# Row 1's causal convolution on TensorE with diagonal matrices, its B/C projection behind the first feature maps

## The chip, the core and the metric

The program runs on one core of a Trainium2 chip. Its engines are TensorE (PE, matrix products into PSUM), VectorE (DVE), ScalarE (ACT), GpSimd (POOL) and SyncE (SP, which here only starts DMAs). Each engine works through its own queue in order; semaphores tie the queues together. The time is the device time of one execution in microseconds (us), and each comparison takes the median of several.

## What is computed

A decoder layer on `x` (4, 512, 512) with three residual parts: linear attention with 16 heads, a selective state-space mixer (as in Mamba) that reads `ctx_1024` (4, 512, 256) and is gated by the normalized `x`, and a feed-forward part with 8-bit activations and ternary weights. The change is in the front of the mixer:

```python
x = jnp.einsum('bld,ed->bel', hidden_states, in_proj_w)            # (4, 512, 512)
xc = conv_general_dilated(x, conv_w, window_strides=(1,), padding=[(3, 0)],
                          feature_group_count=512)                 # 4 taps, one filter per channel
x = silu(xc + conv_b[None, :, None])                               # "U" in the kernel
x_dbl = jnp.einsum('bdl,ed->bel', x, x_proj_w)                     # 16 + 16 + 16 rows
dt_low, Bm, Cm = jnp.split(x_dbl, [16, 32], axis=1)
dt = softplus(jnp.einsum('brl,dr->bdl', dt_low, dt_proj_w) + dt_proj_b[None, :, None])
# scan over time: state = state * exp(dt * A) + (dt * x) * B;  y = (state * C).sum() + D * x
```

## The kernel before

The batch has four rows, b = 0 to 3, and everything is laid out with channels on the 128 partitions and the 512 time steps along them, so that a tensor of 512 channels is four tiles (e = 0 to 3). The mixer's scan is cut into 32 units per row, each for one state n and one half h of the channels: TensorE spreads the row of B over all partitions into PSUM (`spread_b`), VectorE multiplies it by DU (`inputs_b`) and scans (`scan`), ScalarE makes the decays exp(dt A) for it ahead of time (`decay`), GpSimd multiplies by the row of C, adds two units of row 0 together and starts a DMA that accumulates them into ACC (`outputs_c`). These units run through the whole kernel; tables written out by hand (`STEP_PIECES`, `STEP_DECAYS`, `STEP_SPREADS`) say at which named point of an engine's program how many of them are placed. Between them stand the attention of row b (`attention`, four groups g of four heads) and the feed-forward part of row b - 1. In row 0, ScalarE also forms absolute sums of 24 pieces of the feed-forward weights and makes them ternary.

The front of the mixer for row b is: `xin` (the input projection, four products of two 128x512 matmuls each), `tap` on ScalarE (the last tap and the bias, from PSUM into U), `conv` on VectorE (three `scalar_tensor_tensor` per tile, which read the product in PSUM and accumulate in U), `silu_u` on ScalarE, `xdbl` on TensorE (the 48 rows of B, C and the low-rank step size), `x_proj` on ScalarE (which drains them) and, at the end of the row, `step_size` and `step_inputs` (DU = DT x U, on GpSimd). Row 0's front opens the kernel. Row 1's stands in row 0, ahead of its attention: TensorE's `first_row` issues `xin(1, e)`, two spreads, `xdbl(1)` and then `attention(0)`; ScalarE's issues `tap(1, e)`, three decays and two weight sums, `silu_u(1, e)`, a load of the table for exp and ln, `skip_term(1, 0)`, `x_proj(1)` and then `attention(0)`; VectorE's `STEP_PIECES[0]` puts the twelve steps of `conv(1, e)` between units 3 to 5. Rows 2 and 3 have their front inside the feed-forward part of the row before.

Every product has a PSUM bank and two counting semaphores (class `Banks`): TensorE waits until the bank's last reader has drained it. The bank is the one least recently used in the order of `all_products`. DU and the diagonal's input IDF (the identity) and CW (the taps) are in SBUF. ARENA is a scratch region; columns 0 to 2047 of it hold QT, KTT, T1 and T2 of the attention, which nothing writes before the first `first_factor`.

At the start of the kernel GpSimd computes the four tiles of DU of row 0 and then waits for unit 0; VectorE meanwhile cuts B into three bf16 parts (`split_first`, lines 1915 to 1924), normalizes the rows of x (`normed`, line 1879) and begins with the units. The transposes of the normalized rows (`normed_T`, line 916) wait for all four tiles.

Of the kernel before, what the change touches and what calls it, by code (L numbers as in the profile page):

```python
# [19 lines left out]
ALU = mybir.AluOpType  # L20
# [3 lines left out]
P = 128  # L24
# [9 lines left out]
TAPS = 4  # L34
# [88 lines left out]


def front_products(b):
    return [(b, "xin", e) for e in range(KT)] + [(b, "xdbl")]

# [18 lines left out]
def attention_products(b):  # L146

    out = []
    for g in range(first_group(b), GROUPS):
        out += [(b, m, g) for m in ("q1", "q2", "k1", "k2")]  # L150
        if g + 1 < GROUPS:
            out += [(b, "q", g + 1)]
        if g > first_group(b):
            out += [(b, "ms", g - 1)]
        if b + 1 < BATCH and g == 2:
            out += [(b + 1, "dt", 0), (b + 1, "dt", 1)]
        out += [(b, "kfT", g), (b, "S", g, 0), (b, "S", g, 1), (b, "kv", g)]
        if b + 1 < BATCH and g == GROUPS - 1:
            out += [(b + 1, "xnT", k) for k in range(KT)]
        if b == 0 and g == 1:  # L160
            out += [(0, "gsum")]
        if g + 1 < GROUPS:
            out += [(b, "k", g + 1)]
        out += [(b, "o", g), (b, "S", g, 2), (b, "S", g, 3)]
        if g + 1 < GROUPS:
            out += [(b, "v", g + 1)]
    return out
# [341 lines left out]
def decoder_layer(nc, x, ctxT, wqT, wkT, wvT, woT, fmaps, fbias, normw, inT, convw, convb, xpT, dtpT, dtb, alog,  # L509
                  dskip, wffn, ffbias, outb, ident, ident16, id96, causal, headones, out, parts):  # L510
    ctx = ExitStack()
    with ctx:
# [112 lines left out]
        HT = part(3072, 1024, bf16).rearrange("p (k t) -> p k t", k=HK)  # L625
        HALVES = [part(off, 1024) for off in (4096, 5120, 0)]


# [63 lines left out]
        conv_step = signal("conv_step", KT * (TAPS - 2))  # L692
        u_ready = signal("u_ready", KT)
        split_step = signal("split_step", 4)
        bc_parts = signal("bc_parts", 32)
# [32 lines left out]
        hr_ready = signal("hr_ready", 2 * TT)  # L728
        bias_added = signal("bias_added", 1)

        block = ctx.enter_context(nc.Block())
# [138 lines left out]
        def _(pe):  # L870
# [21 lines left out]
            def xin(b, e):  # L892
# [3 lines left out]
                        [ctx_loaded.at(b)])  # L896

            def xdbl(b):
                key = (b, "xdbl")
                product(key, over_k(R.bank(*key)[0:2 * N + RANK, :], [(WXP[:, k, :], U[:, k, :]) for k in range(KT)]),  # L900
                        [u_ready.at(b)])

# [243 lines left out]
            def attention(b):  # L1146
                for g in range(first_group(b), GROUPS):
# [11 lines left out]
                    if b + 1 < BATCH and g == 2:  # L1159
                        step_size(b + 1, 0)  # L1160
                        step_size(b + 1, 1)
                    units(b, "a", g, 2)
                    keys_T(b, g)
# [19 lines left out]
            def first_row():  # L1183
# [19 lines left out]
                units(0, "r", 3)  # L1203
                xdbl(1)
                pe.wait_ge(setup_v, SETUP_V)
# [109 lines left out]
        def _(act):  # L1315
# [4 lines left out]
            def tap(b, e):  # L1320

                act.wait_ge(*R.full_at(b, "xin", e))
                if e == 0 and b:
                    act.wait_ge(*du_ready.at(b - 1))
                act.activation(U[:, e, :], R.bank(b, "xin", e)[:, :], ACT.Identity, bias=CB[:, e:e + 1],  # L1325
                               scale=CW[:, e, TAPS - 1:TAPS]).then_inc(tap_done.sem, 1)

            def silu_u(b, e):
                act.wait_ge(*R.drained_at(b, "xin", e))
                act.activation(U[:, e, :], U[:, e, :], ACT.Silu).then_inc(u_ready.sem, 1)  # L1330
# [47 lines left out]
            def skip_term(b, h):  # L1378

                act.wait_ge(*u_ready.at(b))  # L1380
                if h and b:
                    act.wait_ge(*yg_ready.at(b - 1))
                for i in range(2):
                    e = 2 * h + i
                    act.activation(ACC[(2 * b + h) % 3][:, i, :], U[:, e, :], ACT.Identity, scale=DSK[:, e:e + 1])\
                       .then_inc(y_init.sem, 1)
# [158 lines left out]
            def attention(b, f):  # L1545
                for g in range(first_group(b), GROUPS):
# [19 lines left out]
                    if g == 1 and f is not None:  # L1566
                        act.wait_ge(*R.full_at(f, "O", TT - 1))
                    keys_rows(b, g)
                    decays(b, "a", g, 3)
# [11 lines left out]
            def first_row():  # L1581
# [28 lines left out]
                for e in range(KT):  # L1610
                    tap(1, e)
                decays(0, "r", 3)
# [3 lines left out]
                skip_term(1, 0)  # L1616
                x_proj(1)
                attention(0, None)
# [127 lines left out]
        def _(pool):  # L1746
# [30 lines left out]
            def step_inputs(b, e):  # L1777

                pool.wait_ge(*R.drained_at(b, "dt", e))
                if b:  # L1780
                    pool.wait_ge(*dbu_done.at(0, half_units(b - 1, e // 2)[-1] + 1))
                pool.wait_ge(*u_ready.at(b, e + 1))
                pool.tensor_tensor(DU[:, e, :], DT[:, e, :], U[:, e, :], ALU.mult).then_inc(du_ready.sem, 1)  # L1783

            def split(b):
# [8 lines left out]
                pool.tensor_tensor(BC1, BCR, BC2, ALU.subtract).then_inc(split_step.sem, 2)  # L1794

            for e in range(KT):
                step_inputs(0, e)
            for u in range(TOTAL):
                outputs_c(u)
# [17 lines left out]
        def _(dve):  # L1817
# [80 lines left out]
            def conv(b, e, row=None):  # L1898

                x_in = R.bank(b, "xin", e)  # L1900
                for s in range(1, TAPS):
                    units(row, "c", e, s)
                    if s == 1:
                        dve.wait_ge(*tap_done.at(b, e + 1))
                    else:
                        dve.wait_ge(*conv_step.at(b, e * (TAPS - 2) + s - 1))
                    ins = dve.scalar_tensor_tensor(U[:, e, s:], x_in[:, 0:L - s], CW[:, e, TAPS - 1 - s:TAPS - s],  # L1907
# [522 lines left out]
```

## Time and profile before

| | |
|---|---|
| median of 3 runs | 935.37 us (933.5 to 935.75) |
| the profiled execution | 929.06 us, span 927.3 us |
| TensorE busy | 788.3 us (85%) |
| VectorE busy | 770.0 us (83%) |
| ScalarE busy | 596.8 us (64%) |
| GpSimd busy | 489.6 us (53%) |
| mean granted clock of TensorE | 0.936 |

Busy times overlap, and a wait counts only where nothing else is late at its place. A row of the timeline gives the start, the busy time from there to the end of the last merged instruction, the engine, the line in the kernel, the operation, the tile written and the tiles read, the number of instructions, and in brackets the idle time before it with what ended it. An f32 matmul has two records in the trace, so "x8" of `MATMUL ... f32` are four matmuls. The granted clock 1.00 is 2.4 GHz and 0.50 is 1.2 GHz.

### The profile page before, as it was taken

What the parts mean: (1) busy time and instruction counts of PE and PEld (TensorE: products, weight loads), DVE (VectorE), ACT (ScalarE), POOL (GpSimd) and SP (SyncE); (2) the same over time, 40 slices, a digit from 0 to 9 for tenths busy, and PEclk for the clock granted to TensorE, in tenths of its full rate; (3) what the DMA queues carried; (4) which work ended last, traced back from release to release, by engine and by line L of the source; (5) the groups of instructions that cost most, each with busy time, mean ns of one, the idle gap of its engine ahead of it and who ended that gap; (6) DMA issues with size and microseconds to landing.
All of it is one profiled execution on the core that took longest, in us unless ns stands there. A gap on an engine that the chain in (4) does not pass through costs nothing. (4 is left out here: it accounts for less than half of the span.)

```text
span 927.3 us, 11769 instructions
## 1 busy us (share of the span) xinstructions
PE 788.3 (85%) x4070; PEld 427.9 (46%) x4070; DVE 770.0 (83%) x948; ACT 596.8 (64%) x900; POOL 489.6 (53%) x292
## 2 busy tenths in 40 slices
PE   5859998369788898998987887998889899999798
PEld 1334555143453334665453334655446335664343
DVE  5987778996998985989589988689778998987875
ACT  3888899975746956455466966463466786454553
POOL 0456678787656523575447643276453745565020
PEclk9989997679999999999989999999998999999999
DMA  8697788876545535567635663456653565666000
GB/s 292 255 250 230 213 261 230 236 189 170 121 103 122 114 69 114 138 145 174 127 69 120 121 134 69 125 120 147 159 107 81 117 129 125 153 143 137 0 12 35
DMA packets 50783, 131.12 MB, mean 141 GB/s; under 512 B 7299, under 2 KB 7875, under 8 KB 50725
## 3 DMA queue, kind: packets, MB, share of 16 engines
q0 software_dynamic: 16128, 58.73, 33.5%
q1 hardware_dynamic: 34596, 71.65, 23.9%
q8 instruction: 33, 0.54, 0.2%
q14 instruction: 26, 0.21, 0.1%
HBM read 67.09 MB, written 4.35 MB: 77 GB/s over the span
## 5 line engine op out<-in xcount | busy, mean ns | idle before, releaser
L1762 POOL TENSOR_TENSOR W<-W,CROW 128x1024 f32<-128x1024 f32 x128 | 322.6, 2537 | 158.7 <-DVE W L1951 131.7
L1951 DVE TENSOR_TENSOR_SCAN W<-DEC,PB 128x1024 f32<-128x1024 f32 x125 | 285.1, 2281 | 11.2 <-ACT DEC L1375 3.1
L1775 POOL DMA_DIRECT2D ACC<-W x112 | 98.5, 879 | 153.9 <-DMA ACC<-W 130.2
L1940 DVE TENSOR_TENSOR PB<-DU,PB 128x1024 f32<-128x1024 f32 x128 | 156.5, 1223 | 13.2 <-PE PB L1070 11.6
L1375 ACT ACTIVATE DEC<-DT,ACOL 128x511 f32<-128x511 f32 x250 | 160.1, 711 | 10.3 <-DVE W L1951 10.2
L1126 PE MATMUL bank<-W,ARENA 128*128 128x512 fp8e4 x512 | 125.2, 389 | 0.0
L1318 ACT ACTIVATE ARENA<-bank 128x512 f32<-128x512 f32 x56 | 32.6, 592 | 72.5 <-PE bank L886 34.8
L1126 PEld LDWEIGHTS bank<-W,ARENA 128*128 128x128 bf16 x512 | 45.6, 99 | 61.8 <-issue 17.9
L1479 ACT ACTIVATE ARENA<-bank,SDQ 128x512 f32<-128x512 f32 x64 | 43.2, 686 | 43.4 <-PE bank L1126 43.1
L1070 PE MATMUL PB<-BC,ID 96*128 96x512 bf16 x98 | 38.6, 408 | 34.2 <-DVE W L1951 32.8
L2093 DVE SCALAR_TENSOR_TENSOR ARENA<-bank,SDQ,ARENA 128x512 f32<-128x512 f32 x64 | 47.3, 743 | 17.5 <-PE bank L1126 6.4
L886 PE MATMUL bank<-XNT,WQ 128*128 128x512 f32 x128 | 61.6, 626 | 0.1
L948 PEld LDWEIGHTS bank<-WV,XNT 128*128 128x128 f32 x512 | 60.4, 195 | 2.7 <-issue 2.2
L1983 DVE TENSOR_TENSOR ARENA<-bank,CAUSAL 128x512 f32<-128x512 f32 x64 | 42.5, 680 | 22.3 <-PE bank L987 22.2
L886 PE MATMUL bank<-XNT,WK 128*128 128x512 f32 x128 | 60.0, 613 | 1.2 <-DVE ARENA L1983 1.1
L948 PE MATMUL bank<-WV,XNT 128*128 128x128 f32 x512 | 61.0, 278 | 0.0
L1142 PE MATMUL bank<-W,ARENA 128*128 128x512 fp8e4 x256 | 57.9, 379 | 0.0
L1119 PE MATMUL bank<-BROW,RT 32*128 32x512 bf16 x128 | 29.5, 385 | 22.6 <-DVE ARENA L2093 12.4
L1468 ACT ACTIVATE ARENA<-bank 128x512 bf16<-128x512 int16 x76 | 40.5, 593 | 11.2 <-PE bank L928 11.2
L1907 DVE SCALAR_TENSOR_TENSOR U<-bank,CW,U 128x511 f32<-128x511 f32 (+2 forms) x48 | 35.4, 746 | 14.1 <-ACT U L1325 12.8
L1783 POOL TENSOR_TENSOR DU<-DT,U 128x512 f32<-128x512 f32 x16 | 22.9, 1509 | 45.2 <-ACT DT L1355 45.2
L886 PE MATMUL bank<-ARENA,FM 128*128 128x512 f32 x96 | 45.2, 600 | 0.6 <-DVE LOW L2170 0.4
(185 smaller groups left out, 1339.3 us busy)
## 6 DMA issues: line engine op xcount, KB each, us to landing
ACC<-W POOLq DMA_DIRECT2D x112, 512.0 KB, 4.6
CROW<-c_rows SPq DMA_DIRECT2D x98, 256.0 KB, 3.6
W<-in_wffn SPq DMA_DIRECT2D x27, 512.0 KB, 6.1
X<-in_wffn SPq DMA_DIRECT2D x21, 512.0 KB, 5.4
X<-in_x SPq DMA_DIRECT2D x7, 1024.0 KB, 8.2
out_dram<-X SPq DMA_DIRECT2D x16, 256.0 KB, 2.2
X<-in_ctxT SPq DMA_DIRECT2D x4, 512.0 KB, 5.5
ARENA<-in_x SPq DMA_DIRECT2D x1, 1024.0 KB, 5.5
```

What stands on the lines that cost most here:

```text
L886: last = pe.matmul(o, lhs, rhs, start=start, stop=n == len(terms) - 1)
L948: last = pe.matmul(o[:, t * P:(t + 1) * P], XNT[:, k, t * P:(t + 1) * P], WV[:, k, g * P:(g + 1) * P], start=k == 0, stop=k == KT - 1)
L1126: last = pe.matmul(o, XQT[:, k, t * P:(t + 1) * P], w, start=False, stop=k == KT - 1)
L1142: last = pe.matmul(o, HT[:, k, :], W8[:, 2 * WPC + k // 2, (k % 2) * 512:(k % 2) * 512 + 512], start=k == 0, stop=k == HK - 1)
L1375: last = act.activation(to[:, i, 1:], DT[:, e, 1:], ACT.Exp, scale=ACOL[:, e, n:n + 1])
L1479: act.activation(G[n % 2], R.bank(f, "G", t, c)[:, :], ACT.Silu, scale=SDQ[:, 0, t:t + 1])\
L1762: pool.tensor_tensor(w, w, CROW[k % 2][:, :].unsqueeze(1).broadcast_to([P, 2, L]), ALU.mult)\
L1775: pool.dma_start(ACC[accumulator(u)][:, :, :], w, accum_op=ALU.add).then_inc(y_summed, 16)
L1940: dve.tensor_tensor(into, du, rows, ALU.mult).then_inc(dbu_done.sem, 1)
L1951: dve.tensor_tensor_scan(flat(W[u % 4]), flat(decay_of(u)), flat(PB[:, scan_bank(u):scan_bank(u) + 2, :]), 0.0, ALU.mult, ALU.add).then_in ...
L1983: dve.tensor_tensor(homes(b, g)["st"][c % 2].rearrange("p (h q) -> p h q", h=HPG), R.bank(b, "S", g, c)[:, :].rearrange("p (h q) -> p h q" ...
L2093: dve.scalar_tensor_tensor(h, R.bank(f, "V", t, c)[:, :], SDQ[:, 1, t:t + 1], G[(t * HC + c) % 2], ALU.mult, ALU.mult)\
```

## The change

Row 1's convolution leaves VectorE. Before the first unit, GpSimd multiplies the identity by each tap of each channel: DIAG holds 16 diagonal matrices, in four instructions of 128x512. ScalarE copies the input projection from PSUM to U without tap and bias (`conv_input`). TensorE then forms the convolution of each tile as four f32 products of a diagonal matrix with U, each shifted by one more step, into one PSUM bank. `silu_u` reads that bank and adds the bias in the same instruction. `xdbl(1)` stands on TensorE behind the four feature maps and the `q` projection of group 0 (which is for group 1), and `x_proj(1)` on ScalarE ahead of `keys_rows` of group 0. Rows 0, 2 and 3 are as before.

```diff
+CONV_ON_PE = 1
 def front_products(b):
-    return [(b, "xin", e) for e in range(KT)] + [(b, "xdbl")]
+    out = [(b, "xin", e) for e in range(KT)]
+    if b == CONV_ON_PE:
+        return out + [(b, "conv", e) for e in range(KT)]
+    return out + [(b, "xdbl")]
...
@@ attention_products
+        if b == 0 and g == 0:
+            out += [(1, "xdbl")]
         out += [(b, "kfT", g), (b, "S", g, 0), (b, "S", g, 1), (b, "kv", g)]
...
+        DIAG = part(0, KT * TAPS * P).rearrange("p (e w c) -> p e w c", e=KT, w=TAPS)
...
@@ TensorE
+            def conv(b, e):
+                key = (b, "conv", e)
+                o = R.bank(*key)
+                product(key, [(o[:, s:], DIAG[:, e, TAPS - 1 - s, :], U[:, e, 0:L - s], s == 0) for s in range(TAPS)],
+                        [(diag_made, KT), R.drained_at(b, "xin", e)])
...
@@ attention
+                    if b == 0 and g == 0:
+                        xdbl(1)
                     units(b, "a", g, 2)
                     keys_T(b, g)
...
@@ first_row
                 units(0, "r", 3)
-                xdbl(1)
+                for e in range(KT):
+                    conv(1, e)
                 pe.wait_ge(setup_v, SETUP_V)
                 attention(0)
...
@@ ScalarE
+            def conv_input(b, e):
+                if e == 0:
+                    act.wait_ge(*du_ready.at(b - 1))
+                drain((b, "xin", e), U[:, e, :], R.bank(b, "xin", e)[:, :])
+
             def silu_u(b, e):
+                if b == CONV_ON_PE:
+                    act.wait_ge(*R.full_at(b, "conv", e))
+                    act.activation(U[:, e, :], R.bank(b, "conv", e)[:, :], ACT.Silu, bias=CB[:, e:e + 1])\
+                       .then_inc(R.drained(b, "conv", e), 1)
+                    return
...
@@ attention
+                    if b == 0 and g == 0:
+                        x_proj(1)
                     keys_rows(b, g)
...
@@ first_row
                 for e in range(KT):
-                    tap(1, e)
+                    conv_input(1, e)
                 decays(0, "r", 3)
...
                 skip_term(1, 0)
-                x_proj(1)
                 attention(0, None)
...
@@ GpSimd
+            def diagonals(e):
+                if e == 0:
+                    pool.wait_ge(w_conv, W_CONV)
+                    pool.wait_ge(w_misc, W_MISC)
+                pool.tensor_tensor(DIAG[:, e, :, :], IDF[:, :].unsqueeze(1).broadcast_to([P, TAPS, P]),
+                                   CW[:, e, :].unsqueeze(2).broadcast_to([P, TAPS, P]), ALU.mult).then_inc(diag_made, 1)
             for e in range(KT):
                 step_inputs(0, e)
+            for e in range(KT):
+                diagonals(e)
             for u in range(TOTAL):
...
@@ VectorE, conv
                 for s in range(1, TAPS):
                     units(row, "c", e, s)
+                    if b == CONV_ON_PE:
+                        continue
```

The remaining lines replace waits on `u_ready` of row 1 by waits on the drained banks of its `conv` products, and count the semaphores of the other rows' convolutions without row 1.

## Rows read from the trace of the kernel before

**Rows 1.** Timeline of VectorE, 50 to 81 us (columns as told above).

```profile
50.36 1.23 DVE L1940 TENSOR_TENSOR PB<-DU,PB 128x1024 f32<-128x1024 f32 x1 [2.90 <-PE PB L1070]
...
68.48 2.29 DVE L1951 TENSOR_TENSOR_SCAN W<-DEC,PB 128x1024 f32<-128x1024 f32 x1
...
75.23 0.75 DVE L1970 SCALAR_TENSOR_TENSOR ARENA<-bank,FB,ARENA 128x512 f32<-128x512 f32 x1 [4.47 <-PE bank L886]
...
80.82 1.23 DVE L1940 TENSOR_TENSOR PB<-DU,PB 128x1024 f32<-128x1024 f32 x1 [0.74 <-PE PB L1070]
```

**Rows 2.** Timeline of TensorE's products, 56 to 81 us.

```profile
56.96 0.60 PE L1070 MATMUL PB<-BC,ID 96*128 96x512 bf16 x2
...
67.38 5.84 PE L886 MATMUL bank<-U,WXP 128*48 128x512 f32 x8 [9.82 <-ACT U L1330]
...
73.14 1.98 PE L886 MATMUL bank<-X,FM 128*128 128x512 f32 x4
...
76.90 3.60 PE L886 MATMUL bank<-XNT,WQ 128*128 128x512 f32 x8
...
80.33 0.38 PE L1070 MATMUL PB<-BC,ID 96*128 96x512 bf16 x1
```

**Rows 3.** Stretches: us, busy us of PE, PEld, DVE, ACT, POOL; clock, DMA share, GB/s.

```profile
36.00:51.00 15.00, 13.73 (x69) 8.81 (x68) 11.96 (x9) 14.87 (x27) 9.06 (x4) 1.00 0.58 187
...
61.60:71.80 10.20, 4.42 (x6) 1.17 (x7) 9.03 (x8) 8.28 (x13) 5.15 (x4) 0.50 0.86 231
...
80.00:212.00 132.00, 98.35 (x573) 62.14 (x572) 114.84 (x99) 119.30 (x162) 102.56 (x55) 0.83 0.81 229
...
201.60:211.70 10.10, 5.84 (x21) 2.91 (x22) 8.16 (x6) 7.89 (x8) 7.50 (x4) 0.50 0.75 220
```

**Rows 4.** Timeline of ScalarE, 65 to 75 us.

```profile
65.14 2.19 ACT L1330 ACTIVATE U<-U 128x512 f32<-128x512 f32 x4
...
68.64 1.33 ACT L1385 ACTIVATE ACC<-U,DSK 128x512 f32<-128x512 f32 x2
...
73.74 0.57 ACT L1318 ACTIVATE XBC<-bank 48x512 f32<-48x512 f32 x1
...
74.31 0.69 ACT L1410 ACTIVATE ARENA<-bank,FBS 128x512 f32<-128x512 f32 x1
```

**Rows 5.** Timeline of VectorE, 10 to 36 us.

```profile
10.75 8.99 DVE L1907 SCALAR_TENSOR_TENSOR U<-bank,CW,U 128x511 f32<-128x511 f32 x12 [9.35 <-ACT U L1325]
...
27.68 0.41 DVE L1919 CAST X<-X 32x512 bf16<-32x512 f32 x1
...
28.84 1.25 DVE L1922 COPY BC<-X 32x512 bf16<-32x512 bf16 x1
...
30.10 1.39 DVE L1924 CAST BC<-X 32x512 bf16<-32x512 f32 x1
...
32.98 2.55 DVE L1879 TENSOR_SCALAR ARENA<-ARENA,MV,RSTD 128x512 f32<-128x512 f32 x4 [0.23 <-ACT RSTD L1349]
```

**Rows 6.** Timeline of GpSimd, 28 to 47 us.

```profile
28.46 2.74 POOL L1783 TENSOR_TENSOR DU<-DT,U 128x512 f32<-128x512 f32 x2 [28.02 <-ACT DT L1355]
...
31.17 2.71 POOL L1783 TENSOR_TENSOR DU<-DT,U 128x512 f32<-128x512 f32 x2
...
40.55 5.68 POOL L1762 TENSOR_TENSOR W<-W,CROW 128x1024 f32<-128x1024 f32 x2 [6.67 <-DMA CROW<-c_rows]
```

**Rows 7.** Timeline of VectorE and of GpSimd, 242 to 248 us.

```profile
242.90 3.42 DVE L2165 TENSOR_TENSOR ARENA<-ACC,ARENA 128x1024 f32<-128x1024 f32 x2
...
243.32 4.13 POOL L1783 TENSOR_TENSOR DU<-DT,U 128x512 f32<-128x512 f32 x2 [2.63 <-ACT DT L1355]
```

**Rows 8.** Timeline of TensorE's products, 34 to 40 us.

```profile
35.59 1.97 PE L916 MATMUL bank<-IDF,ARENA 128*128 128x128 f32 x16 [1.02 <-DVE ARENA L1879]
...
39.05 0.39 PE L1070 MATMUL PB<-BC,ID 96*128 96x512 bf16 x1 [1.27 <-DVE W L1951]
```

**Rows 9.** Timeline of VectorE at 216 us.

```profile
216.00 0.69 DVE L1990 TENSOR_TENSOR OT<-bank,OT 128x512 f32<-128x512 f32 x1 [4.97 <-ACT OT L1423]
```

More of the change, by code:

```diff
@@ L122, in quarters, with conv_rows @@
     return (2 * half, 2 * half + 1)
+CONV_ON_PE = 1
 def front_products(b):
-    return [(b, "xin", e) for e in range(KT)] + [(b, "xdbl")]
+    out = [(b, "xin", e) for e in range(KT)]
+    if b == CONV_ON_PE:
+        return out + [(b, "conv", e) for e in range(KT)]
+    return out + [(b, "xdbl")]
+def conv_rows(b):
+    return b - (b > CONV_ON_PE)
 SCALE_GROUPS = ((0, 1), (1, 2), (2, 3), (3, 4))
@@ L693, in decoder_layer @@
         u_ready = signal("u_ready", KT)
+        diag_made = once("diag_made")
         split_step = signal("split_step", 4)
@@ L729, in decoder_layer, with conv_done @@
         bias_added = signal("bias_added", 1)
+        def conv_done(b, n=KT):
+            if b == CONV_ON_PE:
+                return R.all_drained_at(*((b, "conv", e) for e in range(n)))
+            return [u_ready.at(conv_rows(b), n)]
         block = ctx.enter_context(nc.Block())
@@ L900, in xdbl @@
                 product(key, over_k(R.bank(*key)[0:2 * N + RANK, :], [(WXP[:, k, :], U[:, k, :]) for k in range(KT)]),
-                        [u_ready.at(b)])
+                        conv_done(b))
             def step_size(b, e):
@@ L1378, in skip_term @@
             def skip_term(b, h):
-                act.wait_ge(*u_ready.at(b))
+                for r in conv_done(b):
+                    act.wait_ge(*r)
                 if h and b:
@@ L1781, in step_inputs @@
                     pool.wait_ge(*dbu_done.at(0, half_units(b - 1, e // 2)[-1] + 1))
-                pool.wait_ge(*u_ready.at(b, e + 1))
+                for r in conv_done(b, e + 1):
+                    pool.wait_ge(*r)
                 pool.tensor_tensor(DU[:, e, :], DT[:, e, :], U[:, e, :], ALU.mult).then_inc(du_ready.sem, 1)
@@ L1902, in conv @@
                     units(row, "c", e, s)
+                    if b == CONV_ON_PE:
+                        continue
                     if s == 1:
-                        dve.wait_ge(*tap_done.at(b, e + 1))
+                        dve.wait_ge(*tap_done.at(conv_rows(b), e + 1))
                     else:
-                        dve.wait_ge(*conv_step.at(b, e * (TAPS - 2) + s - 1))
+                        dve.wait_ge(*conv_step.at(conv_rows(b), e * (TAPS - 2) + s - 1))
                     ins = dve.scalar_tensor_tensor(U[:, e, s:], x_in[:, 0:L - s], CW[:, e, TAPS - 1 - s:TAPS - s],
```

## The prediction

> **What bounds the kernel now.** I read the changed place first on VectorE, then TensorE, then ScalarE, in the timelines of 50 to 81 us, and after that asked what the new GpSimd work meets in the first 40 us. VectorE is the busiest engine after TensorE, but look at what ends its idle time. It runs the convolution of row 1 between the mixer's units, finishes its last unit of the block at 70.77 us and then stands still for 4.47 us until TensorE has the first feature map [rows 1]. Later it waits 0.74 us for the spread of B of unit 7. TensorE in turn stands still for 9.82 us before the projection to B and C, which then takes 5.84 us for four products [rows 2], since its granted clock is 0.50 (1.2 GHz) from 61.6 to 71.8 us, 4 us into that wait [rows 3]. What ends TensorE's wait is the last `silu_u`, itself behind VectorE's last tap. So a chain convolution (VectorE), SiLU (ScalarE), B/C projection and first map (TensorE) sets this place. ScalarE lies just beside it: a table load (the 1.3 us between its last SiLU and its skip terms) and 1.33 us of skip terms run under the projection, and it comes to `first_factor` at 74.31 us [rows 4].
>
> **What goes.** Twelve VectorE instructions, 8.99 us in row 0's identical convolution [rows 5]. All of them fall before 65 us, in a stretch whose end is a 4.47 us wait for another engine, so by themselves they are worth nothing: without them VectorE's units 4 and 5 are done near 64.5 us (unit 4's spread comes at 57.4, then two products and two scans, 1.23 + 2.29 us each) and it waits some 11 us instead of 4.5.
>
> **What the chain becomes.** A group of four f32 products of 128x512 goes from start to start in 3.43 us at full clock (76.90 to 80.33 us [rows 2]); the new `conv` is four such groups, 511 to 509 columns in three of four, so 13.7 us. The last spreads before it end at 57.4 us, the first input is in U by then (a copy like the one that drains XBC, 0.57 us [rows 4]), so TensorE runs 57.4 to 71.1 us without a gap and at full clock. The last SiLU can start at 71.3 and takes 0.65 us (2.19 for four [rows 4]); the load and the skip terms, formerly hidden under the projection, now follow it: 71.95 + 1.3 + 1.33 = 74.6 us for `first_factor`, against 74.31. VectorE's first map comes at 75.3 instead of 75.23. Nothing is gained there: TensorE is 2 us earlier (71.1 against 73.14), ScalarE 0.3 later, and the later one decides.
>
> TensorE next does the four feature maps (to 74.7 us) and the projection `q` of group 1. It takes the bank of q1, which `first_factor` frees at 75.3 us: 75.3 + 3.43 = 78.7. Then comes the moved projection, 3.43 us at full clock, to 82.15; and only behind it, in TensorE's queue, the spread for unit 7, the transposes of the keys, the scores and kv. Before, that spread started at 80.33 us. VectorE waited for it already (0.74 us), so it is late by 82.15 - 80.33 = **1.8 us**. On ScalarE, `x_proj` (two instructions, 1.1 us) waits for the moved product and holds `keys_rows`, three decays and nine weight sums behind it, 2.2 us late; the first of these decays belongs to unit 8, whose scan lies a whole unit behind the late spread, so 1.8 stays. From 80 to 212 us VectorE is busy for 114.8 of 132 us and ScalarE for 119.3 [rows 3], and what they wait for is on engines that are shifted alike, so I carry 1.8 us to the end. B and C themselves are asked for by `split` behind unit 9 and by the step sizes of group 2: hidden. No DMA moves; `store_c(1)` stands late in the queue of SyncE.
>
> **The diagonals.** GpSimd forms DIAG in four instructions of 128x512 behind its four DU products. It is idle from 33.88 to 40.55 us [rows 6], and four at 1.36 us (2.74 for two) seem to fit. But see what VectorE does there. The same small cast takes 0.41 us alone, and 1.25 and 1.39 us while GpSimd multiplies DU [rows 5, 6]; the two engines take turns. The same at 243 us: two VectorE products of SBUF operands need 3.42 us instead of 2.46 (2 x 1.23, a product of that size [rows 1]), two GpSimd products 4.13 instead of 2.74 [rows 6, 7]. Just where the diagonals start, VectorE normalizes row 0 (`normed`, four TENSOR_SCALAR of 128x512, 2.55 us from 32.98 [rows 5]). Its first one already waits for the last DU. The next three would each find a diagonal in front: from the casts, 0.84 and 0.98 us each; from [rows 7], 3.42 - 2.46 = 0.96. I take three times 1.0, so 3.1 us with hand-over; the bounds are 0 (VectorE always served first) and 3 x 1.31 = 3.9 (a whole GpSimd instruction each).
>
> The Trainium skill says in "GPSIMD Engine Reference", section "Key points", that GpSimd shares its SBUF interfaces with VectorE and collides with instructions in a 2-port mode or with two SBUF inputs; "VectorE: DVE Perf Modes", section "Mode 2×_2P", makes f32 `tensor_scalar` such a one. The trace agrees (0.41 against 1.25 and 1.39 us). Neither gives a price; by them the port term stands, and by GpSimd's idle time alone it would be 0 and the time 937.2.
>
> That delay has no cover. The transposes of row 0 wait for all four normalized tiles, VectorE's first unit is queued behind them, TensorE waits 1.27 us for that first scan at 39.05 us [rows 8], then works through q, k and v without a gap, and VectorE waits 2.90 us for the spread behind v at 50.36 [rows 1]. So 3.1 us pass on to the start of `conv`. TensorE's idle time before the transposes grows from 1.02 to 4.1 us [rows 8]. In the wait from 57.56 us the clock fell after 4 us and stayed at 0.50 for 10.2 us [rows 2, 3]; here too a stretch at 1.2 GHz may come. It costs nothing, or up to 1.7 us if 3.4 us of q and k run at half clock. I take 0.6, nearer to nothing because TensorE works again at once.
>
> **The sum.** 1.8 + 3.1 + 0.6 = 5.5 us. The profiled execution (929.06 us, span 927.3) would become 934.6. It was 0.7% faster than the median of the three runs, 935.37; the shift is the same there: **940.9 us**. With the bounds of the unknown terms: 1.8 + 0 + 0 = 1.8 to 1.8 + 3.9 + 1.7 = 7.4, so 937.2 to 942.8.
>
> **Rivals.**
> - *The diagonals cost nothing.* GpSimd takes its turn only when VectorE asks for none; the four are done before its first C product. For it: two of VectorE's normalizations in a row ran undisturbed, but nothing of GpSimd's was queued then. Then only the moved projection counts: 937.2 us, no change that can be told. It decides where fewer than one of the three turns goes to GpSimd (1.8 + 1.0 = 2.8 us, which is 0.3% and about what a measurement of this kernel can tell from no change).
> - *Given back by the clock.* Row 0's end has a stretch at 0.50 from 201.6 to 211.7 us [rows 3], behind which VectorE waits 4.97 us for the RMS of the last heads [rows 9]. A shifted program meets the clock otherwise; if TensorE is at full speed there, at most 4.97 us come back. With 1.8 that is 932.2 us, faster; with 5.5 it is 935.9. Against it: that stretch begins in waits of TensorE for scans, which the change leaves.
> - *It does less harm or more by ScalarE.* If the copies and SiLUs of row 1 come late behind the normalization's delay (ScalarE is busy for 14.9 of 15 us from 36 to 51 us [rows 3]), the chain grows by another 1 to 2 us: 942.5.
> - *The products take one pass.* If the diagonal products ran at 0.43 instead of 0.86 us each, `conv` would end at 64.3, ScalarE at 70.1 for `first_factor`, and the spread of unit 7 would come 2.6 us early; with the diagonals' 3.1 that is 935.9. Every f32 product of 512 columns in the trace has two records and 0.86 us, so I give it little.
>
> **Chances.** Forecast 0.57 (about 939 to 942.5), diagonals free 0.20, clock gives back 0.11, later ScalarE 0.09, one pass 0.03. Of the clock's 0.11 some 0.07 end faster by over 0.3%, of the forecast's some 0.02 fall within 0.3%. That makes faster 0.07, same 0.28, slower 0.65. The range for 8 in 10 reaches from inside the free and clock cases to the ScalarE case: 935.5 to 943.0.
>
> **What would show it.** Right: `normed` of row 0 with three instructions of 1.4 to 1.6 us each, and the first scan ending near 42.1 instead of 39.05; TensorE without a gap from the four `xin` to the last `conv`, ending 21 us after the first `xin` starts; VectorE idle for about 11 us before its first feature map; the spread of unit 7 behind the moved projection, and 5 to 6 us on the start of row 1. Wrong: `normed` at 2.6 us in all (then 937); `first_factor` far ahead of the last `conv` plus 3.3 us; or row 0's later waits on DMA and ACC sums shrinking by microseconds, which would mean that the shift is absorbed.

## The result, and the profile after

| | before | after |
|---|---|---|
| median (lowest to highest) | 932.02 us (928.72 to 936.99, 18 runs) | 938.05 us (930.37 to 943.76, 18 runs) |
| ratio of after to before | | 1.0067, 95% interval 1.0048 to 1.0085 |
| the profiled execution | 929.06 us, span 927.3 | 943.76 us, span 941.6 |
| TensorE, VectorE busy | 788.3, 770.0 us | 808.0, 767.3 us |

The change makes the kernel some 6 us slower. The forecast was 940.9 us (935.5 to 943.0) and a shift of 5.5 us. The profiled execution of after is the slowest of its 18. VectorE's first unit starts at 40.29 us in it instead of 35.46, and some of that was late before any new instruction ran: DU's first product starts at 29.91 us instead of 28.46 [rows 6]. So the places are compared by intervals from one unit of VectorE to another (u3 is its fourth unit), and the starting stretch by a second series of the same kernel, **change_again**.

First the changed place. Timeline of TensorE after, 55 to 89 us; it answers to [rows 2]:

```profile
55.60 7.03 PE L907 MATMUL bank<-X,WIN 128*128 128x512 f32 x16
...
62.90 13.86 PE L907 MATMUL bank<-U,ARENA 128*128 128x512 f32 x32
76.59 1.88 PE L907 MATMUL bank<-X,FM 128*128 128x512 f32 x4
...
80.84 3.67 PE L907 MATMUL bank<-XNT,WQ 128*128 128x512 f32 x8 [0.43 <-ACT ARENA L1451]
84.45 3.63 PE L907 MATMUL bank<-U,WXP 128*48 128x512 f32 x8
88.01 0.39 PE L1097 MATMUL PB<-BC,ID 96*128 96x512 bf16 x1
```

The second row is the convolution: 16 products, 32 records, 0.86 us each as forecast. No row down to the feature maps has an idle time; in the window below TensorE is busy for all of it, at full clock. Then ScalarE, 76 to 89 us; it answers to [rows 4]:

```profile
76.80 0.69 ACT L1366 ACTIVATE U<-bank,CB 128x512 f32<-128x512 f32 x1 [2.74 <-PE bank L907]
77.50 1.28 ACT L1565 ACT_TABLE_LOAD   x1
78.79 1.33 ACT L1426 ACTIVATE ACC<-U,DSK 128x512 f32<-128x512 f32 x2
80.03 0.67 ACT L1451 ACTIVATE ARENA<-bank,FBS 128x512 f32<-128x512 f32 x1
...
88.12 0.59 ACT L1582 ACTIVATE BC<-bank 32x512 bf16<-32x512 f32 x1 [1.92 <-PE bank L907]
```

The feature maps are long done when ScalarE comes to `first_factor`: last SiLU, table load and skip terms stand in a row, all behind the last product. VectorE, 55 to 89 us; it answers to [rows 1]:

```profile
55.87 1.23 DVE L1995 TENSOR_TENSOR PB<-DU,PB 128x1024 f32<-128x1024 f32 x1 [3.31 <-PE PB L1097]
...
80.73 0.75 DVE L2025 SCALAR_TENSOR_TENSOR ARENA<-bank,FB,ARENA 128x512 f32<-128x512 f32 x1 [10.65 <-ACT ARENA L1451]
...
88.51 1.23 DVE L1995 TENSOR_TENSOR PB<-DU,PB 128x1024 f32<-128x1024 f32 x1 [2.93 <-PE PB L1097]
```

VectorE is rid of 9 us of work and stands still for 10.65 us instead of 4.47. From the spread that starts u3 to the first feature map it takes 24.86 us (55.87 to 80.73); before it was 24.87 (50.36 to 75.23 [rows 1]). From u3 to u7 it takes 32.64 us instead of 30.46. That is the interval on which most of what follows rests, because it holds the whole changed place and starts at the same point in every kernel.

Now the start, in change_again: timelines of VectorE, GpSimd and TensorE, 33 to 46 us. They answer to [rows 5], [rows 6] and [rows 8]:

```profile
33.37 4.71 DVE L1932 TENSOR_SCALAR ARENA<-ARENA,MV,RSTD 128x512 f32<-128x512 f32 x4 [0.23 <-ACT RSTD L1389]
38.01 1.22 DVE L1995 TENSOR_TENSOR PB<-DU,PB 128x1024 f32<-128x1024 f32 x1
```

```profile
34.22 4.76 POOL L1844 TENSOR_TENSOR ARENA<-IDF,CW 128x512 f32<-128x512 f32 x4
```

```profile
38.14 3.48 PE L943 MATMUL bank<-IDF,ARENA 128*128 128x128 f32 x16 [3.04 <-DVE ARENA L1932]
...
42.51 3.67 PE L907 MATMUL bank<-XNT,WQ 128*128 128x512 f32 x8 [0.45 <-ACT XNT L1348]
```

The four normalizations take 4.71 us instead of 2.55, TensorE waits 3.04 us for them instead of 1.02, and its 16 transposes take 3.48 us instead of 1.97. The view of that line, in ns (least, median, most), shows each of them held up:

```profile
L1932 DVE TENSOR_SCALAR ARENA<-ARENA,MV,RSTD x4: 1178/1256/1257, 33.4 to 36.8; 128x512 f32<-128x512 f32 x4
```

The same view of before, where only the first one stands beside GpSimd:

```profile
L1879 DVE TENSOR_SCALAR ARENA<-ARENA,MV,RSTD x4: 533/534/1182, 33.0 to 35.0; 128x512 f32<-128x512 f32 x4
```

A normalization beside nothing adds 0.46 us there ((2.55 - 1.18) / 3; each starts a little before the last has ended). In change_again each of these three adds 1.18 us ((4.71 - 1.18) / 3).

Windows of after; columns as in [rows 3]:

```profile
40.31:43.73 3.42, 3.30 (x16) 3.31 (x17) 3.39 (x3) 1.64 (x3) 0.00 (x0) 0.50 0.30 88
43.73:56.00 12.27, 11.82 (x54) 7.26 (x53) 8.41 (x8) 12.04 (x22) 9.11 (x4) 1.00 0.47 138
55.60:76.80 21.20, 21.20 (x52) 9.51 (x51) 10.54 (x6) 13.49 (x24) 12.68 (x6) 1.00 0.82 232
```

The transposes run at 1.2 GHz behind TensorE's wait (4.18 us in this execution); from the projection q on the clock is whole again.

### The profile page after: what moved, and what is told of

Same layout as the page of the kernel before. It is cut to its first block, busy times and chain, and to the rows that moved or that the text cites. A ratio compares the mean times of both kernels' runs of the same rounds, so it can differ in the third digit from the quotient of the medians.

```text
span 941.6 us, 11838 instructions
## 1 busy us (share of the span) xinstructions
PE 808.0 (86%) x4102; PEld 438.8 (47%) x4102; DVE 767.3 (81%) x936; ACT 596.7 (63%) x900; POOL 493.6 (52%) x296
## 4 chain that ended last, share of the span: by engine, by line
PE 46%; DVE 25%; issue 11%; ACT 9%; POOL 4%; DMA 4%; DVEq 0%; SPq 0%; POOLq 0%; ACTq 0%
PE bank L907 18%; DVE W L2006 8%; PE bank L1153 6%; DVE PB L1995 4%; PE bank L1054 4%; PE bank L975 3%; DMA ACC<-W 3%; PE bank L1169 3%; POOL W L1804 3%; PE bank L1014 2%; PE bank L1037 2%; PE bank L996 2%; DVE HAM L2156 1%; DVE ARENA L2148 1%; PE bank L943 1%
## 5 line engine op out<-in xcount | busy, mean ns | idle before, releaser
L907 PE MATMUL bank<-XNT,WK 128*128 128x512 f32 x128 | 62.1, 631 | 3.2 <-DVE ARENA L2038 3.1
L1054 PE MATMUL bank<-WO,OT 128*128 128x512 f32 x96 | 46.1, 635 | 2.6 <-DVE OT L2045 2.6
```

The costliest lines, as they stand in the source:

```text
L907: last = pe.matmul(o, lhs, rhs, start=start, stop=n == len(terms) - 1)
L1054: pe.matmul(R.bank(*key)[:, :], OT[:, k, t * P:(t + 1) * P], WO[:, k, :], start=k == 0, stop=False, skip_group_check=True)
```

## The experiments

Each kernel ran in five rounds beside the kernel before. There were three series: diag_only, diag_early, pe_later_early and maps_first in the first; change_again, diag_late, move_only and move_later in the second; the rest, on another chip, in the third. "Ratio" is against before of the same series, with its 95% interval, as recorded; it is not the quotient of the two medians and can differ from it by up to 0.002. The medians of before were 931.19, 932.46 and 931.92 us. Intervals are read from VectorE's timeline of one profiled execution.

| kernel | median us | ratio | u0 to u3 | u3 to u7 | u3 to u32 |
|---|---|---|---|---|---|
| before | | | 14.90 | 30.46 | 155.97 |
| after | 938.05 | 1.0067 (1.0048 to 1.0085) | 15.58 | 32.64 | 158.81 |
| change_again | 939.9 | 1.008 (1.0046 to 1.0113) | 15.50 | 32.64 | 158.84 |
| diag_only | 935.52 | 1.0043 (1.0015 to 1.0071) | 15.44 | 30.99 | 158.45 |
| diag_early | 936.66 | 1.0059 (1.0031 to 1.0086) | 14.90 | 32.64 | 159.15 |
| diag_late | 937.47 | 1.0048 (1.0022 to 1.0074) | 14.90 | 32.64 | 158.78 |
| pe_later_early | 936.56 | 1.0056 (1.0035 to 1.0077) | 15.97 | 29.64 | 158.77 |
| pe_stay_early | 936.11 | 1.0037 (1.0012 to 1.0062) | 14.91 | 33.08 | 158.22 |
| conv_short | 930.59 | 0.9983 (0.996 to 1.0006) | 14.99 | 28.21 | 154.31 |
| move_only | 928.07 | 0.9958 (0.9934 to 0.9982) | 14.91 | 28.77 | 152.95 |
| move_only_2 | 930.35 | 0.9975 (0.9953 to 0.9997) | 14.91 | 28.79 | 154.23 |
| move_later | 930.15 | 0.9958 (0.9936 to 0.998) | 14.90 | 25.08 | 156.20 |
| maps_first | 929.41 | 0.9983 (0.9963 to 1.0004) | 16.09 | 28.10 | 154.29 |
| maps_first_warm | 931.1 | 0.9987 (0.9962 to 1.0013) | 15.92 | 27.89 | 153.87 |

**diag_only.** The kernel before with the four diagonal products at the place of the change; nothing reads them.

```diff
             for e in range(KT):
                 step_inputs(0, e)
+            for e in range(KT):
+                diagonals(e)
```

> The kernel before plus the four GpSimd instructions for the diagonals, at the place where the change puts them; nobody reads them (ScalarE only waits for them before the attention), and the convolution stays on VectorE. My theory: they take turns with VectorE's normalization, which lasts 5 to 6 us instead of 2.55, TensorE goes idle for 4 us, and the time is 3 to 4 us above the kernel before (ratio 1.003 to 1.005). Rival (GpSimd is idle there, so they cost nothing): ratio 1.000.

The normalizations again take 4.71 us:

```profile
33.88 4.71 DVE L1892 TENSOR_SCALAR ARENA<-ARENA,MV,RSTD 128x512 f32<-128x512 f32 x4 [0.23 <-ACT RSTD L1351]
```

The time is 1.0043 of before. Four instructions that no one needs cost about 4 us (1.4 to 6.6 by the interval), and the profile shows 2.7 of them: 2.16 in the normalizations and 0.54 from u0 to u3, where the transposes ran at half clock. "Diagonals cost nothing" falls. The ratio is the expected one, but the four normalizations (4.71 us) and TensorE's wait (3.04 us) are below the 5 to 6 and the 4 us expected. This profile is also 0.53 us longer from u3 to u7 and 1.95 from there to u32 than that of before, where the edit adds nothing but a wait that has long been met; what takes these 2.5 us was not followed up.

**diag_early** and **diag_late.** The change with the diagonals ahead of DU, while GpSimd waits for DT; and with GpSimd waiting for `normed` before them.

```diff
-            for e in range(KT):
-                step_inputs(0, e)
             for e in range(KT):
                 diagonals(e)
+            for e in range(KT):
+                step_inputs(0, e)
```

```diff
                     pool.wait_ge(w_conv, W_CONV)
                     pool.wait_ge(w_misc, W_MISC)
+                    pool.wait_ge(*xn_ready.at(0))
```

> The changed kernel with the four diagonals ahead of the four DU products instead of behind them, where VectorE normalizes nothing. My theory: the 3 to 4 us of the turns go, the moved projection's 1.8 to 2.2 us stay: ratio to the kernel before 1.002 to 1.0025. Rival (all of the loss is in the moved projection and the convolution): ratio stays at 1.006 to 1.007.

> The changed kernel, with GpSimd waiting for the four normalized tiles before its first diagonal, so that nothing takes turns. The diagonals early left a ratio of 1.006, more than my sum had. Theory A (the turns cost 3 us, and the rest of the change 2.2 us as the spread of unit 7 shows; the ratio of the early diagonals lay high within its uncertainty): ratio 1.002 to 1.004, and unit 7 2.2 us later against unit 3 than in the kernel before. Theory B (the convolution on TensorE and the moved projection cost some 5 us in all, part of it later in row 0): ratio 1.005 to 1.006 again.

Timelines of VectorE of diag_early, and of VectorE and GpSimd of diag_late:

```profile
34.05 2.54 DVE L1932 TENSOR_SCALAR ARENA<-ARENA,MV,RSTD 128x512 f32<-128x512 f32 x4 [0.23 <-ACT RSTD L1389]
```

```profile
33.67 2.54 DVE L1933 TENSOR_SCALAR ARENA<-ARENA,MV,RSTD 128x512 f32<-128x512 f32 x4 [0.23 <-ACT RSTD L1389]
36.14 1.21 DVE L1996 TENSOR_TENSOR PB<-DU,PB 128x1024 f32<-128x1024 f32 x1
```

```profile
36.38 4.04 POOL L1845 TENSOR_TENSOR ARENA<-IDF,CW 128x512 f32<-128x512 f32 x4 [1.82 <-DVE ARENA L1933]
```

In both the last three normalizations are undisturbed and u0 to u3 is 14.90 us as before. In diag_late GpSimd multiplies beside VectorE's products and scans, and VectorE's 1.21 us product and u0 to u3 do not grow. That product reads DU from SBUF and PB from PSUM. The Trainium skill ("GPSIMD Engine Reference", section "Key points") names as contending VectorE's instructions in a 2-port mode or with two SBUF inputs; this trace agrees, with one SBUF input and no loss here. diag_late is 2.4 us faster than change_again, its neighbour on the same chip (939.9 against 937.47; the two intervals overlap), where the profile has 2.76 us (2.16 + 0.60). So by the profiles the place of the diagonals is worth 2 to 3 us. The ratios of the change with and without turns don't separate it: 1.0067 and 1.008 against 1.0059 and 1.0048, all intervals overlapping. Both kernels remain at 1.005 to 1.006, about 5 us that are not the turns'. The expectation of diag_early (1.002 to 1.0025) missed this, and that of diag_late is split: unit 7 is 2.18 us late as in theory A, the ratio is nearer to theory B.

**move_only**, **move_only_2.** The kernel before with nothing but the moved projection, the convolution on VectorE; two series.

```diff
@@ attention, TensorE
+                    if b == 0 and g == 0:
+                        xdbl(1)
                     units(b, "a", g, 2)
@@ first_row, TensorE
-                xdbl(1)
@@ attention, ScalarE
+                    if b == 0 and g == 0:
+                        x_proj(1)
                     keys_rows(b, g)
@@ first_row, ScalarE
-                x_proj(1)
```

> Only the second half of the change: the convolution stays on VectorE and there are no diagonals, but row 1's B/C projection and its drain stand where the change puts them (behind the q projection). Theory A (the loss of the change at this place is the 13.7 us chain of products followed by SiLU, table load and skip terms, and the move by itself gains): VectorE gets its first map without a wait, unit 7 is 2 to 2.5 us earlier against unit 3, ratio 0.997 to 0.999. Theory B (it is the moved projection ahead of the spread of unit 7 that loses): 1.8 to 2.2 us slower, ratio 1.002.

> The kernel before with nothing but the projection to B and C moved to the place of the change (TensorE: behind the feature maps and the q projection; ScalarE: ahead of the rows of the keys); a second series of the same kernel, beside the others of this call. Theory A (the move by itself gains 3 to 4 us, since the first feature maps no longer wait for a projection at half clock): ratio 0.994 to 0.998. Rival B (the first series was chance): 0.999 to 1.001.

Timelines of move_only, TensorE, and of move_only_2, VectorE:

```profile
68.05 3.62 PE L888 MATMUL bank<-X,FM 128*128 128x512 f32 x4
71.46 4.08 PE L888 MATMUL bank<-XNT,WQ 128*128 128x512 f32 x8
75.47 3.63 PE L888 MATMUL bank<-U,WXP 128*48 128x512 f32 x8
79.04 0.39 PE L1072 MATMUL PB<-BC,ID 96*128 96x512 bf16 x1
```

```profile
71.12 0.72 DVE L1974 SCALAR_TENSOR_TENSOR ARENA<-bank,FB,ARENA 128x512 f32<-128x512 f32 x1
...
75.22 0.72 DVE L1974 SCALAR_TENSOR_TENSOR ARENA<-bank,FB,ARENA 128x512 f32<-128x512 f32 x1
79.58 1.23 DVE L1944 TENSOR_TENSOR PB<-DU,PB 128x1024 f32<-128x1024 f32 x1 [3.63 <-PE PB L1072]
```

The moved projection alone makes the kernel faster: 0.9958 and 0.9975, some 2 to 4 us, both intervals below 1. The first feature map comes with no wait and 4.5 us earlier (20.33 us behind u3, 71.12 - 50.79, instead of 24.87). Of that 2.9 are lost again at the spread of unit 7, which now stands behind the projection (3.63 us of waiting), and 1.7 us stay (30.46 - 28.78), somewhat less than the 2 to 2.5 expected. The projection now takes 3.63 us instead of 5.84; the slow stretch has gone over to the two feature maps and to q (3.62 and 4.08 us). This is one half of the change, and the better half.

**move_later**, **pe_later_early.** The projection one step further down, behind the projection k of group 1: once with the convolution on VectorE, once with it on TensorE (diagonals early).

```diff
                         qk(b, "k", g + 1)
+                    if b == 0 and g == 0:
+                        xdbl(1)
                     attend(b, g, 0)
```

> The kernel before with row 1's B/C projection moved further, behind the k projection of group 1; convolution on VectorE, no diagonals. Theory A: the spread of unit 7 comes right behind the q projection, VectorE's wait for it (2.95 us with the maps first) goes, and the projection costs 1.5 us at unit 10: 3 to 4 us faster than before, ratio 0.996 to 0.997. Rival (the projection delays the second pair of scores as much as it gave back): ratio 0.998, as with the maps first.

> As diag_early, and row 1's B/C projection moved on from ahead of the keys' transposes to behind the k projection of group 1 (its drain on ScalarE alike), where TensorE waits 1.7 us for a masked score. My theory: the spread of unit 7 is no longer behind the projection, so VectorE reaches it up to 0.6 us earlier than in the kernel before, the projection costs about 1 us later: ratio 1.000 to 1.001. Rival (the convolution on TensorE itself delays the chain, wherever the projection stands): as diag_early or above, 1.002.

VectorE no longer waits for the spread of unit 7, and u3 to u7 falls to 25.08 and 29.64 us, 3.7 and 3.0 us less than with the projection at the place of the change. The ratios gain nothing: 0.9958 and 1.0056, as their partners have (pe_later_early was expected at 1.000 to 1.001, a miss). In the profile of move_later the interval from u7 to u12 is 23.00 us instead of before's 21.05, and that from u12 to u32 108.11 instead of 104.45. Of the first, 1.5 us lie at the spread of unit 10, which stands behind the projection now, as expected (u9 to u10 6.48 us instead of 5.01):

```profile
89.88 1.23 DVE L1944 TENSOR_TENSOR PB<-DU,PB 128x1024 f32<-128x1024 f32 x1 [2.46 <-PE PB L1072]
```

So in this profile the gain at unit 7 is handed back before row 1; what takes the rest was not isolated. One execution does not carry the median here: this one has a longer u3 to u32 and a longer span (928.3 us) than the profiled execution of before (927.3), while the ratio over 12 runs is 0.9958.

**maps_first**, **maps_first_warm.** The kernel before with the projection between the four feature maps and the projection q; the second with 34 small products that keep TensorE busy in its wait.

```diff
                     units(b, "a", g, 1)
+                    if b == 0 and g == 0:
+                        xdbl(1)
                     if more:
                         qk(b, "q", g + 1)
```

> The kernel before with only its order changed: the convolution stays on VectorE, the B/C projection of row 1 goes behind the four feature maps of group 0 and ahead of the q projection, its drain on ScalarE alike; no diagonals. My theory: VectorE no longer waits 4.5 us for the first map, and the projection runs in TensorE's idle time; the spread of unit 7 comes 2.3 us earlier than before (TensorE at 1.2 GHz for part of it): ratio 0.997 to 0.998. Rival (the gain of an earlier first map is lost because TensorE then does projection and q in a row): ratio 1.000.

> The kernel before with the projection to B and C between the four feature maps and the projection q of group 1, the convolution on VectorE, and 34 keep-busy products of TensorE ahead of the feature maps, in its wait for the last spreads. Theory A (the half clock of the projection behind a wait of 9.8 us costs here): the maps and the projection run at 1.00, unit 3 to 7 is 1 to 2 us shorter than the 28.1 us without the keep-busy products, ratio 0.994 to 0.997. Rival B: the wait for SiLU ends later than the products and the clock is not what decides: ratio as without them, 0.998.

0.9983 and 0.9987: neither can be told from before, and they differ by 0.0004. The keep-busy products do what they should, the last two maps run faster (1.88 us instead of 3.29), but unit 7 gains 0.2 us only (28.10 to 27.89):

```profile
60.23 7.51 PE L878 MATMUL bank<-IDB 128*128 128x512 bf16 x34 [1.04 <-DVE U L1911]
...
68.66 1.88 PE L888 MATMUL bank<-X,FM 128*128 128x512 f32 x4
71.45 3.60 PE L888 MATMUL bank<-U,WXP 128*48 128x512 f32 x8 [0.91 <-ACT ARENA L1413]
```

The 0.91 us in front of the projection say why: TensorE is early and waits for ScalarE to free a bank. Theory A fell; a faster clock just here is worth next to nothing. The projection itself had little to gain here, it takes 3.63 us in maps_first too. Whether a full clock would help the kernel before, in which the projection stands ahead of the maps and takes 5.84 us, no run tried.

**pe_stay_early.** The change, diagonals early, with the projection left directly behind the convolution.

```diff
                 for e in range(KT):
                     conv(1, e)
+                xdbl(1)
                 pe.wait_ge(setup_v, SETUP_V)
```

> The change with the diagonals ahead of DU and with the projection to B and C left where it was before, directly behind row 1's convolution. Theory A (with the convolution on TensorE, ScalarE's table load and skip terms are as late as the projection, so its place hardly matters): the first feature map comes 0.5 to 1.5 us later, the spread of unit 7 within 1 us of the change's, interval unit 3 to 7 32.5 to 34 us, ratio 1.005 to 1.008. Rival B (the move is worth its 4 us here too): interval 36 to 37 us and ratio about 1.010.

Timeline of TensorE, then of ScalarE:

```profile
73.69 3.60 PE L905 MATMUL bank<-U,WXP 128*48 128x512 f32 x8 [0.98 <-ACT U L1363]
77.22 1.98 PE L905 MATMUL bank<-X,FM 128*128 128x512 f32 x4
```

```profile
73.45 1.28 ACT L1562 ACT_TABLE_LOAD   x1
74.75 1.34 ACT L1423 ACTIVATE ACC<-U,DSK 128x512 f32<-128x512 f32 x2
77.33 0.59 ACT L1579 ACTIVATE BC<-bank 32x512 bf16<-32x512 f32 x1 [1.25 <-PE bank L905]
```

The first feature map comes 2.6 us later than with the projection moved (27.49 us behind u3 instead of 24.87), more than the 0.5 to 1.5 expected, but in exchange unit 7 waits only 0.74 us for its spread. So u3 to u7 is 33.08 us, 0.44 more, and the ratio is 1.0037 against 1.0059, intervals overlapping. With the convolution on TensorE the move is worth next to nothing: the load and the skip terms (2.6 us) fill most of the projection's time, and ScalarE waits for it for 1.25 us only. Rival B (4 us here too) falls; the ratio came out a little below what theory A gave (1.005 to 1.008).

**conv_short.** The change, diagonals early, with one of the four products per tile.

```diff
-                product(key, [(o[:, s:], DIAG[:, e, TAPS - 1 - s, :], U[:, e, 0:L - s], s == 0) for s in range(TAPS)],
+                product(key, [(o[:, s:], DIAG[:, e, TAPS - 1 - s, :], U[:, e, 0:L - s], s == 0) for s in range(1)],
```

> The change with the diagonals ahead of DU and with only one of the four tap products per tile on TensorE (taps 0 to 2 of row 1 are left out, so row 1 and what follows from it is another number). Everything else of the change stays: diagonals, copies, SiLU from PSUM, the moved projection. TensorE's convolution is 3.4 us instead of 13.7. Theory A (the length of the products is what the change pays at unit 7): VectorE's interval from unit 3 to unit 7, 32.64 us in the change, falls to 28 to 29 as in the kernel with the move alone, and the median goes to 0.995 to 0.999 of before. Rival B (the price lies in copies, banks or in what the diagonals leave behind): the interval stays above 31 us or the ratio stays at 1.004 to 1.006.

```profile
59.54 3.60 PE L907 MATMUL bank<-U,ARENA 128*128 128x512 f32 x8
67.93 3.42 PE L907 MATMUL bank<-X,FM 128*128 128x512 f32 x4 [4.79 <-ACT U L1366]
```

With 3.6 us of convolution on TensorE instead of 13.9, TensorE stands still for 4.79 us before the feature maps, u3 to u7 is 28.21 us (4.43 less than diag_early) and the time 0.9983 of before, against 1.0059. Everything else of the change is in this kernel. So the length of the 16 products is what the change pays in the middle; no cost of copies, SiLU from PSUM, banks or the space for DIAG shows. By the ratios the length is worth more than by this interval: 0.0076, some 7 us. It lands beside move_only and maps_first, in which VectorE does the convolution. Of the two numbers expected, the interval was met and the ratio lies in theory A's band of 0.995 to 0.999.

**change_again.** The change itself, a second time, beside diag_late and move_only.

> The changed kernel itself, on the same chip as the next three, so that they can be compared with it. Both theories: ratio 1.005 to 1.008, as first measured.

1.008, with 1.0067 the first time: the loss is there twice.

## Why the prediction was right, step by step

The forecast shift was 5.5 us, the measured ones 6.2 us (0.0067 x 932; 4.5 to 7.9 by the interval) and 7.5 (0.008 x 932). The forecast time of 940.9 us lies 2.9 above the median of 938.05 although the shift was not forecast too large, since it was added to 935.37, a median of three runs; 18 runs give 932.02. Where the profiles put it, change_again against before, adding up to the difference of their spans (934.7 - 927.3): start to u0 2.55 us (2.16 in the normalizations, 0.39 ahead of them), u0 to u3 0.60, u3 to u7 2.18, u7 to u32 0.69, u32 to the end 1.4. The three terms of the forecast cover 2.16, 0.60 and 2.18, so 4.9 us in this execution; for the other 2.5 it has no term. That the sum came out so near is in part luck: the turns were put 0.9 us too high, and costs that nobody foresaw lie on the other side. Without the turns, the forecast's own terms give about 2 us, and diag_early and diag_late measured 5.

- **What goes is worth nothing.** Right. 9 us of VectorE's work became 6.2 us more of its wait, and the first map came 24.86 us behind u3 instead of 24.87.
- **The chain of `conv`.** Right in each piece. 20.99 us from the first `xin` to the first map (forecast 21), 16 products with no gap at full clock, then SiLU, load and skip terms. The forecast had `first_factor` 0.3 us later than before by this chain; it came 0.2 later (24.16 us behind u3 against 74.31 - 50.36 = 23.95).
- **The moved projection, 1.8 us.** Measured 2.18. The forecast counted 3.43 us from group to group; from q to the projection it was 3.61 (80.84 to 84.45) and from the projection to the spread 3.56. With 0.11 us more between `first_factor` and q that is 0.42, against 0.08 less in `first_factor`. The sum along the chain was right, the term 0.4 too small. Its name was not: inside the change the move costs nothing at unit 7, since with the projection left in its old place u3 to u7 is 0.44 us longer still (pe_stay_early), and with one product per tile instead of four it is 4.43 us shorter (conv_short). The 2.18 us belong to the length of the convolution.
- **The turns, 3.1 us.** Mis-sized. Three turns of 1.0 us, 3.1 with hand-over, were priced from the casts (0.84 and 0.98) and from [rows 7] (0.96); each costs 1.18 - 0.46 = 0.72, so 2.16. The sign given for it, three normalizations of 1.4 to 1.6 us, missed too: they show 1.26. A normalization at its undisturbed size still starts every 0.46 us in the kernel before, because the next one begins before the last has ended; the forecast compared durations. It also took 1.36 us for a diagonal, the duration of a DU product; undisturbed the four need 1.01 each (diag_late, 4.04 us). The mechanism, one GpSimd product in front of each of three normalizations, is what the trace shows, and diag_only, diag_early and diag_late show it by switching it on and off.
- **The clock, 0.6 us.** Right in size, by luck, since it was a pick between 0 and 1.7: the half clock took the 16 transposes (3.48 us for 1.97), not q, and 0.54 to 0.68 us stay from u0 to u3 in all three kernels with the turns. As a cost of the turns it is less sure. Of the ten other kernels in the table (without before) seven have 14.90 to 14.99 us there, but three without turns (pe_later_early, maps_first, maps_first_warm) have 15.92 to 16.09, so the half clock comes to this place without them too.
- **"Given back by the clock".** Fell: row 0's end has its stretch at 0.50 as before (change_again: 206 to 216 us), and VectorE waits 5.68 us for the RMS instead of 4.97 [rows 9].
- **ScalarE later, one pass.** Neither: `conv` never waited for an input, and every product took two records and 0.86 us.

What the forecast did not see is the division of the change into halves of opposite sign. It judged the move by what comes late at unit 7 in the whole change, and never asked what the move does alone. By itself it gains 2 to 4 us, because it takes a projection of 5.84 us, most of it at half clock [rows 2, 3], from in front of the first feature map; the convolution on TensorE fills that very time with 13.9 us of products and ends the gain. From u3 to u7 the convolution costs 32.64 - 28.78 = 3.9 us against the move alone, of which the move had brought 1.7. Over the whole kernel it costs more: diag_late's median is 9.4 us above move_only's, of the same series.

**What stays open.** diag_early, diag_late and pe_later_early stand at 1.0048 to 1.0059, some 5 us, of which 2.2 are seen from u3 to u7 in the first two. The rest lies in pieces under 1 us behind it (diag_late: 0.6 from u7 to u32, 0.6 from u32 to u127, 0.85 behind that, 0.7 ahead of u0). Single executions of before scatter from 926.78 to 938.67 us in one series, and u3 to u32 differs by 1.3 us between two executions of one kernel (move_only: 152.95 and 154.23). The lower ends of the ratios' intervals, 1.0031 and 1.0022, are 2.9 and 2.1 us, so a cost of 2.2 us with no further cause is at their edge. The profile of diag_only has u3 to u32 2.5 us longer than before although the edit does nothing there, so such a piece in one profile can't be laid to the convolution. No run here isolates a cause for more, nor for the 5.5 us of the 9.4 between diag_late and move_only that do not lie from u3 to u7.

## What to carry to other kernels

Before work is moved to the engine that stands still, ask what it waits for: TensorE's 9.8 us of waiting were the time in which VectorE made its input, and when TensorE makes it instead, in 13.9 us, the chain is as long as before. Price an "idle" GpSimd by what VectorE does in the same microseconds, and put setup work where VectorE waits or scans; by the profiles that was 2 to 3 us here, and diag_only shows by its median that the wrong place costs. A change with two parts should be measured in parts: here the move alone beats both kernels (0.9958 and 0.9975), and nobody would have seen it from the sum.

## What the runs showed of the hardware

- VectorE's f32 TENSOR_SCALAR of 128x512 and GpSimd's f32 product of 128x512 took strict turns: 1.18 us for a pair, so 0.72 us for each turn given to GpSimd. In the profile both instructions show some 1.2 us at the same time (VectorE alone 0.53, GpSimd's diagonals alone 1.04), so each record seems to hold the wait for the other. The durations of the casts, 1.25 and 1.39 us for 0.41, would have made it 0.84 and 0.98.
- The turns hit small instructions too. In the profiled execution of after, the scaling of ACOL (128x64) stood beside a diagonal:

```profile
35.47 0.86 DVE L2285 TENSOR_SCALAR ACOL<-ACOL 128x64 f32<-128x64 f32 x1 [2.54 <-ACT ACOL L1638]
36.24 4.13 DVE L1932 TENSOR_SCALAR ARENA<-ARENA,MV,RSTD 128x512 f32<-128x512 f32 x4
```

  0.86 us for an instruction that takes 0.19 alone; the four diagonals are then used up one normalization earlier, and the four take 4.13 us instead of 4.71.
- Beside u0's product and scan the same four GpSimd instructions cost VectorE nothing that shows (diag_late: 1.21 us for the product, u0 to u3 14.90 us).
- The wait right before it does not say what clock TensorE gets. Behind waits of 3.04 us (change_again, diag_only) the transposes ran at half clock for most of their time, 3.48 and 3.42 us; behind 0.88 and 0.89 us (diag_late, diag_early) at full clock, 1.97 us; but behind 0.88 us in pe_later_early they took 3.68 us.
